# Down projection in three passes over rounded halves, with k, v and r kept in the scan buffers

## The reference

```python
h = einsum(w0[inputs], w1) * mask * 16                  # gather 512-wide rows, project to 256
# RWKV block on layernorm(h)
k, v, r = mixk @ wk, mixv @ wv, sigmoid(mixr @ wr)      # 256 -> 256 each
x = x + (r * wkv_scan(k, v, time_decay, time_first)) @ wo
kk = square(relu(mixk2 @ cwk))                          # 256 -> 1024
x = x + sigmoid(mixr2 @ cwr) * (kk @ cwv)               # 1024 -> 256
# FFN on layernorm(h), every operand quantised to a 4-bit grid in blocks of 16
gate, y = xq @ w_gate_q.T, xq @ w_up_q.T                # 256 -> 704
out = h + quant(silu(gate) * y) @ w_down_q.T            # 704 -> 256, the down projection
```

## Time and profile before

| | |
|---|---|
| median of 3 runs | 747.94 us (747.89 to 749.3) |
| the profiled execution | 747.51 us |
| its span in the profile | 745.7 us |
| TensorE (PE) busy | 716.9 us, 96% |
| VectorE (DVE) busy | 589.2 us, 79% |
| ScalarE (ACT) busy | 510.0 us, 68% |
| GpSimd (POOL) busy | 154.9 us, 21% |

### The profile page before, as it was taken

How to read it: one execution, slowest core, us unless ns; L and a number is a source line. 1 busy time by engine, 2 the same in 40 slices (tenths; PEclk the granted TensorE clock), 3 DMA queues, 4 the chain that set the end, 5 groups by cost and what they waited for, 6 DMA issues and landing times.

```text
span 745.7 us, 10723 instructions
## 1 busy us (share of the span) xinstructions
PE 716.9 (96%) x3702; PEld 602.9 (81%) x3702; DVE 589.2 (79%) x1031; ACT 510.0 (68%) x893; POOL 154.9 (21%) x220
## 2 busy tenths in 40 slices
PE   6998899899999999999999999999999999899987
PEld 5858767797789968897789868896889878898876
DVE  0687969786988789787998799787998698883685
ACT  2674997488858896589757995689748885663231
POOL 2304401430034201530043201620052002200200
PEclk9999999999999999999999999999999999999999
DMA  4801100100002000100011000100010000000000
GB/s 128 286 2 29 29 0 2 28 30 1 15 9 63 1 1 15 43 29 1 15 41 31 1 1 15 56 16 1 14 43 1 1 14 1 15 1 15 15 1 29
DMA packets 13377, 19.39 MB, mean 26 GB/s; under 512 B 982, under 2 KB 10764, under 8 KB 13324
## 3 DMA queue, kind: packets, MB, share of 16 engines
q1 hardware_dynamic: 10720, 10.31, 4.3%
q0 software_dynamic: 2560, 8.39, 3.8%
q10 hardware_dynamic: 44, 0.01, 0.0%
HBM read 14.51 MB, written 4.19 MB: 25 GB/s over the span
## 4 chain that ended last, share of the span: by engine, by line
PE 78%; DVE 11%; ACT 5%; issue 3%; DMA 1%; POOL 1%; DVEq 0%; ACTq 0%; POOLq 0%
PE psB L570 20%; PE psC L645 15%; PE psB L600 11%; PE psC L672 10%; PE psA L561 9%; PE psA L531 6%; PE psC L660 2%; PE psA L519 1%; PE psC L504 1%; DMA rows<-L_tok_w,ids_now 1%; DVE mix L1000 1%; PE psB L541 1%; DVE mix L1025 1%; PE psC L629 1%; DVE scales L1180 1%
## 5 line engine op out<-in xcount | busy, mean ns | idle before, releaser
L570 PE MATMUL psB<-cwv_s,kkT 128*128 128x256 f32 x512 | 113.2, 379 | 0.7 <-ACT kkT L858 0.7
L570 PEld LDWEIGHTS psB<-cwv_s,kkT 128*128 128x128 f32 x512 | 96.6, 190 | 16.8 <-issue 2.9
L561 PE MATMUL psA<-mix,kvr_s 128*128 128x512 f32 x192 | 86.4, 593 | 3.0 <-DVE mix L1000 1.8
L645 PE MATMUL psC<-up_hi,xq_hi 128*128 128x352 f32 x256 | 85.9, 335 | 2.1 <-DVE xq_lo L1273 1.5
L452 POOL TENSOR_SCALAR sc_c<-mv_c 128x2 f32<-128x2 f32 x16 | 7.6, 474 | 384.7 <-DVE mv_c L1163 384.7
L672 PE MATMUL psC<-downT,hqT 128*128 128x256 f32 x384 | 85.9, 380 | 0.1
L645 PE MATMUL psC<-up_hi,xq_lo 128*128 128x352 f32 x256 | 82.6, 323 | 0.0
L645 PE MATMUL psC<-up_lo,xq_hi 128*128 128x352 f32 x256 | 82.5, 322 | 0.0
L672 PEld LDWEIGHTS psC<-downT,hqT 128*128 128x128 f32 x384 | 72.2, 190 | 10.3 <-ACT hqT L923 0.5
L561 PEld LDWEIGHTS psA<-mix,kvr_s 128*128 128x128 f32 x192 | 36.1, 190 | 40.3 <-issue 36.3
L1000 DVE SCALAR_TENSOR_TENSOR mix<-hT,rest,mix 128x512 f32<-128x512 f32 x80 | 54.5, 748 | 16.3 <-ACT mix L774 16.3
(11 more groups left out here) (170 smaller groups left out, 1561.6 us busy)
## 6 DMA issues: line engine op xcount, KB each, us to landing
out<-h SPq DMA_DIRECT2D x16, 256.0 KB, 2.1
mix<-L_attn_cwk SPq DMA_DIRECT2D x1, 1024.0 KB, 10.4
cwv_s<-L_attn_cwv SPq DMA_DIRECT2D x1, 1024.0 KB, 13.2
hq<-L_ffn_w_gate SPq DMA_DIRECT2D x1, 704.0 KB
hq<-L_ffn_w_up SPq DMA_DIRECT2D x1, 704.0 KB, 6.7
hqT<-L_ffn_w_down SPq DMA_DIRECT2D x1, 704.0 KB, 10.2
w_s<-L_tok_w SPq DMA_DIRECT2D x1, 512.0 KB, 3.6
rows<-L_tok_w,ids_now POOLq DMA_INDIRECT x32, 4.0
```

The costliest lines, as they stand in the source:

```text
L561: mm = nc.tensor.matmul(psA[:, A.slot(f"{name}{d}")], kvr_s[:, w, k, d * P:(d + 1) * P], mix[:, w, k].rearrange("p c t -> p (c t)"), start ...
L570: mm = nc.tensor.matmul(psB[:, B.slot(name), q * D:(q + 1) * D], lhsT[:, k, (2 * j + q) * P:(2 * j + q + 1) * P], weight[:, k, :], start=( ...
L645: mm = nc.tensor.matmul(psC[:, C.slot(name), f, 0:INTER // 2], a[:, k, t * P:(t + 1) * P], b[:, w, k, f * (INTER // 2):(f + 1) * (INTER // ...
```

## The change

1. The down projection takes three passes over rounded halves, as the key and up projections do: `down_hi`, `down_lo`, `hqT_hi`, `hqT_lo`, with 18 matmuls of 256 columns for a tile where 6 stood.
2. New steps on VectorE make the low halves: `c_low0` to `c_low3` in every chunk, `w_low` once. The jobs `hq0` to `hq3` are now emptied by VectorE. ScalarE's copy of a transposed tile takes two instructions where it took three.
3. k, v and r no longer have buffers: `kT`, `vT`, `rT` are views of `take`, `takev` and `top`. The normed rows of stage A go to the buffer of the gathered rows. Waits are moved accordingly: the gather waits for `n1`, `norm_a` for `xt3`, the copies of k, v and r for the scan's steps. In the scan, `newv` comes ahead of `takev`.
4. `raw_down` is two tiles with a transfer each, in `h1` and `normc`; the first uses of those wait for the transposes of the weight.
5. All of `ORDER` is new, and `WARM` has 359 transposes.

The diff, cut to its core:

```diff
 ORDER = {
-    "pe": [("w_turn1", 2), ("b_key1", 2), ("a_k", 1), ("b_key2", 2), ("a_v", 1), ("b_key3", 2), ("w_turn2", 2),
-        ("c_down0", 3), ("w_turn0", 1), ("a_r", 1), ("b_value0", 2), ("c_turn2", 3), ("a_turn0", 0),
-        ("b_value1", 2), ("c_turn3", 3), ("c_down1", 3), ("b_out0", 1), ("c_cols0", 2), ("b_out1", 1),
-        ("a_emb0", 0), ("c_up0", 2), ("a_turn1", 0), ("c_cols1", 2), ("b_cols", 1), ("a_emb1", 0), ("c_up1", 2),
-        ("b_gate", 1), ("c_turn0", 2), ("c_up2", 2), ("b_key0", 1), ("a_cols", 0), ("c_turn1", 2), ("w_par", -16),
-        ("c_up3", 2)],
+    "pe": [("c_up2", 2), ("a_cols", 0), ("c_turn1", 2), ("b_key1", 1), ("c_up3", 2), ("a_k", 0), ("b_key2", 1),
+        ("a_v", 0), ("b_key3", 1), ("c_down0", 2), ("w_turn2", 1), ("c_turn2", 2), ("a_r", 0), ("b_value0", 1),
+        ("c_turn3", 2), ("w_par", -6), ("a_turn0", -1), ("w_turn0", 0), ("b_value1", 1), ("c_down1", 2),
+        ("b_out0", 0), ("c_cols0", 1), ("b_out1", 0), ("c_up0", 1), ("a_emb0", -1), ("c_cols1", 1), ("b_cols", 0),
+        ("a_turn1", -1), ("c_up1", 1), ("a_emb1", -1), ("b_gate", 0), ("c_turn0", 1), ("w_turn1", 0),
+        ("b_key0", 0)],
...
+    "dve": [("c_sq3", 2), ("a_wkv2", 0), ("a_wkv3", 0), ("c_down0", 2), ("c_rq3", 2), ("w_low", 1), ("c_low2", 2),
+        ("b_value0", 1), ("c_stat0", 1), ("w_key", 0), ("a_wkv4", 0), ("c_low3", 2), ("c_sn0", 1), ("b_value1", 1),
+        ("c_rn0", 1), ("c_stat1", 1), ("w_split0", 0), ("c_down1", 2), ("c_split0", 1), ("b_x1", 0), ("c_sn1", 1),
+        ("c_up0", 1), ("w_quant1", 0), ("c_rn1", 1), ("c_sq0", 1), ("c_split1", 1), ("w_par", -9), ("b_mix", 0),
+        ("c_rq0", 1), ("a_stat", -1), ("b_low", 0), ("w_quant2", 0), ("c_up1", 1), ("w_quant0", -1), ("c_sq1", 1),
+        ("c_low0", 1), ("c_rq1", 1), ("c_up2", 1), ("c_sq2", 1), ("c_low1", 1), ("a_mix", -1), ("c_rq2", 1),
+        ("a_wkv1", -1), ("c_up3", 1), ("w_split1", 0)],
...
-WARM = {("w_par", 0): 10, ("a_turn0", 0): 14, ("a_cols", 0): 60, ("a_k", 0): 44, ("a_turn0", 1): 24, ("b_out0", 0): 92,
-        ("b_cols", 0): 33, ("c_cols0", 0): 34, ("c_up0", 6): 32, ("c_up0", 7): 24, ("c_turn1", 7): 13, ("c_turn3", 7): 21}
+WARM = {("w_par", 0): 10, ("a_turn0", 0): 14, ("a_cols", 0): 60, ("a_k", 0): 44, ("a_turn0", 1): 10, ("b_out0", 0): 92,
+        ("b_cols", 0): 33, ("c_cols0", 0): 28, ("c_cols1", 6): 28, ("c_cols1", 7): 20, ("c_turn3", 7): 20}
...
-        downT = sb("downT", [P, KI, D])
+        down_hi = sb("down_hi", [P, KI, D], F32R)
+        down_lo = sb("down_lo", [P, KI, D], F32R)
...
+        norm = rows[:].rearrange("p q (t d) -> p (q t) d", d=D)
...
+        kT, vT, rT = [t[:, :, :, 1:ROW] for t in (take, takev, top)]
...
-                        A.wait_full(pool, ch.back(1), "xt3")
+                        A.wait_full(pool, ch.back(1), "n1")
...
                         for k in range(KI):
-                            mm = nc.tensor.matmul(psC[:, C.slot(name), 0, q * D:(q + 1) * D], hqT[:, q, k, :],
-                                                  downT[:, k, :], start=(k == 0), stop=(k == KI - 1))
+                            for p, (a, b) in enumerate(((hqT_hi, down_hi), (hqT_hi, down_lo), (hqT_lo, down_hi))):
+                                mm = nc.tensor.matmul(psC[:, C.slot(name), 0, q * D:(q + 1) * D], a[:, q, k, :], b[:, k, :],
+                                                      start=(k == 0 and p == 0), stop=(k == KI - 1 and p == 2))
...
-                nc.scalar.copy(dst[:, 0:4, :], ps[:, slot, 0].rearrange("p (k n) -> p k n", k=4))
-                nc.scalar.copy(dst[:, 4, :], ps[:, slot, 1, 0:P])
-                nc.scalar.copy(dst[0:TAIL, 5, :], ps[0:TAIL, slot, 1, P:2 * P]).then_inc(last, 1)
+                nc.scalar.copy(dst[:, 0:KI - 1, :], full_blocks(ps, slot))
+                nc.scalar.copy(dst[0:TAIL, KI - 1, :], ps[0:TAIL, slot, 1, P:2 * P]).then_inc(last, 1)
...
+            def lows(slot, lo, hi):
+
+                nc.vector.tensor_tensor(lo[:, 0:KI - 1, :], full_blocks(psC, slot), hi[:, 0:KI - 1, :].bitcast(F32), ALU.subtract)
+                return nc.vector.tensor_tensor(lo[0:TAIL, KI - 1, :], psC[0:TAIL, slot, 1, P:2 * P],
+                                               hi[0:TAIL, KI - 1, :].bitcast(F32), ALU.subtract)
...
+            def low_c(t):
+
+                def step(ch):
+                    at(dve, c_turned, ch, t + 1)
+                    lows(C.slot(f"hq{t}"), hqT_lo[:, t % 2], hqT_hi[:, t % 2]).then_inc(c_dve.sem, 1)
+                return step
```

More of the change, by code:

```diff
@@ L169 @@
 C_JOBS = [("q0", "dve"), ("g0", "act"), ("u0", "dve"), ("q1", "dve"), ("g1", "act"), ("u1", "dve"),
-          ("hq0", "act"), ("g2", "act"), ("u2", "dve"), ("hq1", "act"), ("g3", "act"), ("u3", "dve"), ("d0", "dve"),
-          ("hq2", "act"), ("hq3", "act"), ("d1", "dve")]
-WKV = ["pad", "padv"] + [f"{step}{d}" for step in ("top", "gain", "now", "takev", "sumv", "sum1", "newv", "numer",
+          ("hq0", "dve"), ("g2", "act"), ("u2", "dve"), ("hq1", "dve"), ("g3", "act"), ("u3", "dve"), ("d0", "dve"),
+          ("hq2", "dve"), ("hq3", "dve"), ("d1", "dve")]
+WKV = ["pad", "padv"] + [f"{step}{d}" for step in ("top", "gain", "now", "newv", "takev", "sumv", "sum1", "numer",
                                                    "denom", "near", "fix", "avg", "att")
                          for d in range(H)]
-EXPS = [f"{step}{d}" for step in ("rise", "fall", "keep", "take", "new", "log", "inv") for d in range(H)]
+EXPS = [f"{step}{d}" for step in ("rise", "fall", "new", "keep", "take", "log", "inv") for d in range(H)]
 QUANT = 7
@@ L278, in build @@
         square = sb("square", [P, 2, INTER], F32R)
-        hqT = sb("hqT", [P, 2, KI, P])
+        hqT_hi = sb("hqT_hi", [P, 2, KI, P], F32R)
+        hqT_lo = sb("hqT_lo", [P, 2, KI, P], F32R)
         def flat(t):
@@ L400, in _ @@
                 sp.dma_start(raw_up[:, k * GJ:(k + 1) * GJ, :], w.rearrange("n (h d) -> (n h) d", h=H).rearrange("(j p) d -> p j d", p=P)).then_inc(s_raw[k], 16)
-            sp.dma_start(raw_down, w_down.rearrange("(h p) n -> p h n", p=P)).then_inc(s_raw[2], 16)
+            for h in range(H):
+                sp.dma_start(raw_down[h], w_down[h * P:(h + 1) * P, :]).then_inc(s_raw[2], 16)
             sp.dma_start(raw_key, cwk.rearrange("(k p) d -> p k d", p=P)).then_inc(s_raw[3], 16)
@@ L748, in norm_a @@
                 at(act, a_coef, ch, 4)
-                at(act, wkv, ch.back(1), WKV.index("gain1") + 1)
+                A.wait_full(act, ch, "xt3")
                 for t in range(TILES):
@@ L786, in project @@
             def project(name):
-                dst, last = {"k": (kT, "gain"), "v": (vT, "newv"), "r": (rT, None)}[name]
+                dst = {"k": kT, "v": vT, "r": rT}[name]
                 def step(ch):
+                    if name == "r":
+                        at(act, wkv, ch, WKV.index("gain1") + 1)
+                    elif name == "v":
+                        B.wait_emptied(act, ch.back(1), "o1")
+                    else:
+                        at(act, wkv, ch.back(1), len(WKV))
                     for d in range(H):
                         A.wait_full(act, ch, f"{name}{d}")
-                        if name == "r":
-                            B.wait_full(act, ch.back(1), "o1")
-                        else:
-                            at(act, wkv, ch.back(1), WKV.index(f"{last}{d}") + 1)
-                        nc.scalar.activation(dst[:, d].rearrange("p c t -> p (c t)"), psA[:, A.slot(f"{name}{d}")],
+                        nc.scalar.activation(dst[:, d], psA[:, A.slot(f"{name}{d}")].rearrange("p (c t) -> p c t", t=T),
                                              ACT.Sigmoid if name == "r" else ACT.Copy).then_inc(a_act.sem, 1)
@@ L1058, in wkv_a, with f_newv @@
                 both(1, f_now)
+                def f_newv(d):
+                    A.wait_emptied(dve, ch, f"v{d}")
+                    expd(f"new{d}")
+                    A.wait_full(dve, ch, "v1")
+                    return tt(numer[:, d], e_new[:, d], vT[:, d], ALU.mult)
+                both(2, f_newv)
                 def f_takev(d):
-                    A.wait_emptied(dve, ch, f"v{d}")
                     expd(f"take{d}")
-                    return tt(takev[:, d, :, now], take[:, d, :, now], vT[:, d], ALU.mult)
+                    return tt(vT[:, d], take[:, d, :, now], vT[:, d], ALU.mult)
                 both(2, f_takev)
@@ L1072, in wkv_a @@
                 both(2, lambda d: nc.vector.tensor_tensor_scan(long(take, d), long(keep, d), long(take, d), 0.0, ALU.mult, ALU.add))
-                def f_newv(d):
-                    expd(f"new{d}")
-                    A.wait_full(dve, ch, "v1")
-                    return tt(numer[:, d], e_new[:, d], vT[:, d], ALU.mult)
-                both(2, f_newv)
                 def f_numer(d):
-                    after(f"newv{d}")
+                    after(f"sumv{d}")
                     return tt(numer[:, d], numer[:, d], takev[:, d, :, before], ALU.add)
@@ L1251, in step @@
```

(14 more changed lines are left out.)

60 lines of the change are left out of this document (31 added, 29 removed), and 20 rows, old and new, of the table ORDER.

## The result

The changed kernel takes 739.58 us (median of 4 runs), the kernel before 748.62 us beside it (4 runs): ratio 0.9881, 95% interval 0.9866 to 0.9895, so 9.0 us faster. The forecast was 731 us, 17 us faster, with a range of 723 to 744. The direction and the range held; nearly half of the gain is missing. The profiled execution took 738.6 us, its span is 736.5.

A forecast was written before the change was run, and what follows sets the result against it. TensorE alone was taken to bound the five middle turns, queue order both ends. Terms -15.7 + 3.8 - 1.0 - 4.5 - 1.3 + 0.4 + 1.0 + 0.3 = -17.0 took the span from 745.7 to 728.7, forecast 731 us, range 723 to 744.

The forecast's parts named there:

- Three passes, 16 x 0.98 = 15.7 us: Down projection on TensorE: a step takes 4.20 us instead of 5.18, 0.98 less, over 16 steps 15.7 us less.
- The rival that the weight load isn't hidden: TensorE's down projection: an FP32R instruction needs 0.160 us instead of 0.117, giving 756 us; chance 0.11.
- The new wait at `b_cols`, +3.8, and the up step, -1.0: TensorE's turns: a new wait of 0.75 us, five times, +3.8; first up step no longer waits 0.2 for `c_split0`, -1.0.
- Low halves, 4.0 us a turn, hidden: VectorE's low steps: 1.0 us a tile, 4.0 a turn, hidden if nothing in TensorE's queue waits for them.
- The slack of 0 at `c_low3`: `c_down1` on TensorE waits for VectorE's `c_low3`, ready just as TensorE gets there: no slack, no wait, 0.
- the rival counted by sums over a turn: VectorE becomes the bound: its waits shrink too little for 4.0 us more work; 744 to 763 us; chance 0.16.
- The rest of the edits, 0: Views for k, v, r, ScalarE's two copies, split transfer, later gather, `newv` ahead of `takev`: cost nothing.
- The fill, -4.5: While the pipeline fills: weight copies early, 28 warm transposes in 3.1 us, first `c_cols0` near 136 us; -4.5, ends 0 and -5.5.
- The last part, -5.5: From the start of chunk 6's `b_out1` to the end: six down steps, with -1.3, +0.4, +1.0 and +0.3.
- while it drains: Last turn with scan work: `c_split0` first moves `b_cols` and `b_gate` up 2.3 us, 1.0 already counted: -1.3.
- +0.4 and +0.3: Last turn, while draining: two low steps in the VectorE and ScalarE chain, +0.4; last down step behind a low step, +0.3.
- The full gain, 726 or 723 us: Rival: the new wait at `b_cols` is covered and only streaming counts, 726 us, or 723 with the best fill; chance 0.10.

The follow-up runs named there:

- e10_both_plain: `e3_both` with the down projection in plain 32-bit, the low halves made but not used: 749.43 us, ratio 1.0025 to the kernel before.
- e3_both: The changed kernel with GpSimd's `c_coef0` ahead of `gather1` and the second half of a chunk's output stored from `rr`: 733.84 us.
- e5_low_tail: `e3_both` with each low step cut to its 64x128 part after the first chunk: 732.36 us, ratio 0.979 to the kernel before.
- e1_coef_first: The changed kernel with GpSimd's `c_coef0` ahead of `gather1`: 735.17 us, ratio 0.9823 to the kernel before.
- e4_plain_down: The changed kernel with the down projection in plain 32-bit, the low halves made but not used: 749.55 us, ratio 1.0015 to the kernel before.
- e7_old_lists: The changed kernel's code with the lists and warm transposes of the kernel before, new steps placed: 788.23 us, ratio 1.0531 to the kernel before.

## Why the prediction was right, and where it was off

- **Three passes, 16 x 0.98 = 15.7 us.** Right. `c_down0` takes 4.25 us and `c_down1` 4.10, against 4.20 forecast (0.118 and 0.113 us an instruction; why they differ no run shows); with the waits gone, `e10_both_plain` against `e3_both` gives 15.6 us. The rival that the weight load isn't hidden is refuted: with a load of its own an instruction runs in 0.118 us or less. The Trainium skill (TensorE: Matmul & The Clock Gate, "What overlaps and what doesn't") would make it load plus streaming; the measured 0.118 us decide against that rule for these instructions. That page's columns / 1.2 for a load, 107 ns, is consistent with it, since it still fits; the load proper was measured nowhere.
- **The new wait at `b_cols`, +3.8, and the up step, -1.0.** The step that failed. The forecast's net price was 0.55 us a turn over 82.21 - 1.96 = 80.25. The changed kernel pays 81.37 - 80.25 = 1.12. A wait of the forecast's size is there, 0.73 at `c_cols1`, one step ahead of `b_cols`; the 0.32 at `c_cols0` was not counted at all. I followed the chain to `b_cols` over `b_sum`, took its inputs as ready, and never compared GpSimd's list: there the new order puts `gather1` ahead of `c_coef0`, two issues of 1 us on the path to `c_cols0`; and I said that behind the later gather stood only statistics "a third of a turn away", which is the mistake in words. The wait of `b_sum` for the store was missed as well. With both out of the way the turn is 80.78, and the net price 0.53 is what was forecast, in part by luck: what is left at `c_cols1` is 0.44 us (3.89 against 3.45), not 0.75, and the up steps' gain of 0.27 us a turn is spent again on small differences of other steps.
- **Low halves, 4.0 us a turn, hidden.** Size right (VectorE 73.31 of 81.36 us), hidden in the turn right (`e5_low_tail`: no change). The slack of 0 at `c_low3` didn't become a wait; but the room is far smaller than the rival counted by sums over a turn: 3 us more cost 1.26 a turn. VectorE is not the bound in the changed kernel, and is nearly so.
- **The rest of the edits, 0.** No run takes the views, the later gather or the split transfer apart. In the turns TensorE has no wait for any of them. In the fill the first `a_r` waits 2.38 us for ScalarE's copy of v where it waited 1.18 before, and the lowered clock at 44 to 55 us, where there is one, begins behind this wait.
- **The fill, -4.5.** Mis-sized: -1.84 in the profiled execution, -2.6 in `e3_both`, -4.0 in `e10_both_plain`. As forecast, no lowered clock is left at the warm transposes (28 in 3.22 us) and the weight copies are out of the way; but the first `c_cols0` starts at 139.24, not near 136:

```profile
139.24 0.66 PE L636 MATMUL psC<-ident,normc 128*128 128x128 f32 x4 [0.42 <-DVE normc L1212]
```

  What was left out is the clock elsewhere in the fill. Against `e10_both_plain` the changed kernel is 1.8 us later already behind the first `a_emb1` (23.77 against 21.94): the second half of the gathered rows comes 0.4 us later, four transposes take 0.45 more and `a_emb1` 1.0 more at the lowered clock. The other 0.3 us of the 2.1 at mark 1 is the wait of 0.42 us above: GpSimd's gather ahead of `c_coef0` holds here too, and the kernels with the order turned (`e1_coef_first`, `e3_both`) don't wait there. Of the 0.5 us that `e10_both_plain` still lacks, 0.3 is its lowered clock at `a_r`; the rest isn't settled.
- **The last part, -5.5.** Measured -3.39, and nearly all of the missing 2.1 us is lost before the last `b_gate`. From mark 6 to there it took 651.27 - 552.41 = 98.86 us before and takes 644.09 - 546.60 = 97.49 now: 1.4 less, where the terms give 3.3 (the 2.3 of "while it drains" and the 0.98 of the `c_down0` ahead of it). I gave the new wait to five turns, but the sixth has it too: 0.66 us at `c_cols1` (556.80), 0.44 at `c_cols0` (627.28) and, in the turn behind, 0.86 at `c_cols1` (637.49). Behind the last `b_gate` it is 94.43 us before and 92.41 now, 2.0 less against 2.2 forecast, and this is luck: two terms were wrong and cancel. With a plain down projection (`e4_plain_down`, 96.40) this piece is 2.0 us longer than before, where I had +0.4 and +0.3; and the four down steps in it give 4.0 us, all of them, where I had taken 1.0 away as hidden. `e5_low_tail` shows the share of the low halves: 0.4 us in the sixth turn and 0.6 behind `b_gate`, where the waits for `hqT_lo` fall from 2.4 to 0.9 us and those for `hq` grow from 1.7 to 2.8; what else makes the plain drain longer isn't settled. The last down steps are as forecast:

```profile
720.03 4.25 PE psC L680 x36
...
728.72 4.49 PE psC L680 x36
```

- **The full gain, 726 or 723 us.** This rival's sum doesn't come out: 731 less 3.8 is 727, and 726 with the best fill. The lower end of the range rested on it; the measured time lies far above.

The fastest version run is `e3_both`, 733.84 us, 1.9% under the kernel before and 0.7% under the changed one. `e5_low_tail` is shorter only by leaving work out.

## What to carry to other kernels

When a list is made anew, compare it engine by engine, the least busy engine first: GpSimd, idle for 81% of the span, cost a quarter of what a turn saved, by two gathers ahead of four small instructions. A wait that is covered by a slow engine is part of the price of making that engine faster: look one chain behind the bound for what ends within the time to be saved. And count an engine's room along the stretch on which the next wait hangs, not over a turn.

## What the runs showed of the hardware

- FP32R with 256 columns runs at 0.113 to 0.118 us an instruction with a load of its own, 0.44 to 0.46 ns a column beside the 0.456 of the 352- and 512-column rows. The load itself, estimated at 0.108 us from the rows, still fits.
- A TensorE wait in steady work can lower the granted clock: in `e7_old_lists` 4.73 us of waiting were followed by instructions at 0.21 us instead of 0.12.
- In the fill the place of the lowered clock differs between kernels that have nearly the same work there: 16 to 24 and 48 to 55 us in the changed kernel, 84 to 88 us in `e3_both`, about 44 to 52 us in `e10_both_plain`. Mark 1 of these three lies within 2.1 us. A wait of 2.1 us ahead of `b_gate` was followed by a lowered clock in `e3_both` (0.63) and not in the changed kernel (1.00).
- A tensor_reduce and a tensor_tensor over the same 128x640 in PSUM take VectorE the same 0.82 us.
